# Second attention: the value products of a key tile in two halves by queries, one half in each step, and the output copies one step later

## The chip, the cores and the metric

The kernel runs on one core of a Trainium2 chip. The metric is the device time of one launch in microseconds. TensorE is called PE (its weight loads PEld), VectorE DVE, ScalarE ACT, GpSimd POOL, and SyncE SP; SP and ACT also issue DMAs.

## The reference

Two layers over x of 4 x 512 tokens with 256 features, in fp32. Each layer is x + attention(xn) + ffn(xn), with xn the layer-normalised x. Layer 0 has single-head attention and a mixture of 16 experts (4 per token) with a shared one; layer 1 has the grouped attention below and a mixture of 7 experts (3 per token) with a shared one. The change is in the second attention alone:

```
fused = x @ w_qkv.T + b_qkv            # q: 32 heads of 8; k, v: 8 groups of 8, 4 heads to a group
sim   = einsum('bgrsd,bgtd->bgrst', q, k) / sqrt(8)
attn  = softmax(sim, axis=-1)          # 512 queries x 512 keys, for 4 x 8 groups of 4 heads
out   = einsum('bgrst,bgtd->bgrsd', attn, v)
out   = out.reshape(B, S, 256) @ w_out.T + b_out
```

## The kernel before, in words

Every engine has its own hand-written program; semaphores order them. A unit u is one batch and one group of four heads (4 x 8 = 32 units, NG = 8 units to a batch). The work on a unit is spread over three stages, so that in stage u PE computes the scores of unit u (for their maxima), the transposed scores of unit u-1 (and the last three of u-2), and value products of units u-2 and u-1. A stage has eight steps i, one for each pair of heads in a tile of 128 queries or keys (QT = 4 tiles, 2 pairs).

In each step, in this order on PE:

- `scores_t` (L846): two 32-row products of 512 columns into two PSUM banks, keys by queries, with the maxima folded into the queries (`qm`). ACT's `exponentials` (L1200) turns the two banks into half a tile of `pt`. It runs LAG = 3 steps behind, so steps 0 to 2 still do unit u-2.
- `scores` (L834): two 32-row products of 512 columns into two banks, queries by keys; DVE's `reduce_max` (L1691) takes the maxima out.
- in step 1 `maxima_t` (L873): four 128 x 128 transposes of the negated maxima; DVE then adds them to the queries of the next unit (L1694, gives b_qm). scores_t of unit u-1 begins in step 3 and waits for that.
- in steps 0, 2 and 4 `values` (L858) of the key tiles 1, 2, 3 of unit u-2, and in step 6 of tile 0 of unit u-1: four products of all 128 keys by 512 queries, one for each head, side by side in column groups of 32, accumulated in PSUM bank 7. `va` holds the values with a column of ones, so a row of sums comes out as well.
- in step 3 a projection of the next batch in the stages u % 8 = 5, 6, 7 of all batches but the last (`project`, L563 to L565, six products of 512 columns); ACT (L1179 to L1184) and DVE (L1653, L1656) `compact` it, ACT in its step 4, DVE in step 5.
- in step 4 of stages 9, 17 and 25 `values_by_key` (L823), four transposes, which DVE copies to `va` (L1660).
- in step 6 `outputs_t` (L866): four transposes of `ot`, from which DVE normalises the result (L1668, L1670).

ACT's `outputs` (line 1191, recorded at the helper's line L1000) copies bank 7 to `ot` in ACT's step 4, when the value products of unit u-2 are complete. outputs_t waits for it (b_ot), and so do the first value products of the next unit, which overwrite bank 7.

The banks of both kinds of scores come from a ring of three slots of two banks: `next_slot` lets the n-th use wait for the reader of the use three before. So scores(i) waits for the exponential of scores_t(i-1), and scores_t(i) for the reduction of scores(i-2). PSUM bank 6 (SMALL) is shared by maxima_t, project, values_by_key and outputs_t: `small_bank` lets each wait for the reader of the one before. `pt` is a ring of three key tiles: `exponentials` waits on b_pv until the products of the tile three before are complete.

SP's `stack_keys` and `stack_queries` (L392, L407) bring keys and queries of later units into place by DMA, waiting on b_st and b_qm; POOL scatters tokens to the experts (L482), three scatters for each maxima_t in stages 13 to 28. In stages 3 to 7, 9 and 10 DVE also does the routing of layer 1.

Of the kernel before, what the change touches and what calls it, by code (L numbers as in the profile page):

```python
# [8 lines left out]
B, S, H = 4, 512, 256  # L9
# [3 lines left out]
QT = S // P  # L13
# [16 lines left out]
NG, R, HD = 8, 4, 8  # L30
# [11 lines left out]
def program(nc, x_in, aw0_in, aw1_in, ws0_in, moe0_in, moe1_in, pad_in, const_in, bias_in, out):  # L42
# [3 lines left out]
    with ctx:  # L46
        i32, u32 = mybir.dt.int32, mybir.dt.uint32

        def place(name, col, shape, dt=f32):
            return nc.alloc_sbuf_tensor_at(name, shape, dt, offset=SBUF0 + 4 * col)  # L50

        def sem(name):
            return ctx.enter_context(nc.semaphore(name))
# [76 lines left out]
        psum = ctx.enter_context(nc.psum_tensor("psum", [P, 8, 512], f32))  # L130
# [64 lines left out]
        va = tf(QT, NG, 32)  # L195
        pt = [tf(R, S), tf(R, S), place("pt2", M + 32848, [P, R, S])]
# [60 lines left out]
        b_pv, b_ot, b_ox, b_rc, b_on, b_nt = (sem(n) for n in ("b_pv", "b_ot", "b_ox", "b_rc", "b_on", "b_nt"))  # L257
# [34 lines left out]
        UNITS, PAIRS, LAG = B * NG, 2 * QT, 3  # L292
# [3 lines left out]
        def projects(u):  # L296

            return NEXT.get(u % NG) if u < UNITS - NG else None

        def new_values(u):  # L300

            return u % NG == 1 and NG < u < UNITS
# [258 lines left out]
        def _(pe):  # L561
# [276 lines left out]
            def scores_t(u, i):  # L838

                t, h = i // 2, i % 2  # L840
                if i == 0:
                    pe.wait_ge(b_qm, u + 1)
                bank = next_slot(pe, ("scores_t", u, i), b_ex, u * PAIRS + i + 1)
                for r in range(2):
                    rows = slice(32 * (2 * h + r), 32 * (2 * h + r) + 32)
                    ins = nc.tensor.matmul(psum[:, bank + r, :], km[u % 4][rows, t * P:(t + 1) * P],  # L846
                                           qm[u % 2][rows, :], start=True, stop=True, tile_position=(32 * (2 * h + r), 0))
                ins.then_inc(b_st, 1)

            def values(u, t):  # L850

                pe.wait_ge(b_ex, u * PAIRS + 2 * t + 2)
                if t == 0 and u >= 1:
                    pe.wait_ge(b_ot, u)
                if t == 0 and u % NG == 0:
                    pe.wait_ge(b_va, u // NG + 1)
                for r in range(R):
                    ins = nc.tensor.matmul(psum[32 * r:32 * r + 32, 7, :], va[:, t, u % NG, :], pt[(u * QT + t) % 3][:, r, :],  # L858
                                           start=(t == 0), stop=(t == QT - 1), tile_position=(0, 32 * r))
                ins.then_inc(b_pv, 1)  # L860

            def outputs_t(u):
# [15 lines left out]
            def stage(u, early={}):  # L878

                front = u < UNITS  # L880
                if front:
                    pe.wait_ge(b_kd, (u + 1) * R * 16)
                    pe.wait_ge(b_qd, (u + 1) * R * 16)
                for i in range(PAIRS):
                    if i < LAG and u >= 2:
                        scores_t(u - 2, PAIRS - LAG + i)
                    if i >= LAG and 1 <= u <= UNITS:
                        scores_t(u - 1, i - LAG)
                    if front:
                        scores(u, i)  # L890
                    if i == 1 and 1 <= u <= UNITS:
                        maxima_t(u - 1)
                    if i % 2 == 0 and i < 6 and u >= 2:
                        values(u - 2, 1 + i // 2)
                    if i == 3 and projects(u) is not None:
                        project(projects(u), u // NG + 1, small_bank(pe, b_lo, u // NG * 3 + u % NG - (NG - 3) + 4))
                    if i == 4 and new_values(u):
                        values_by_key(small_bank(pe, b_va, u // NG + 1))
                    if i == 5 and u == NG:
                        prefix(1, small_bank(pe, m_tot, layers(1, 1)))  # L900
                    if i == 6 and 2 <= u <= UNITS:
                        outputs_t(u - 2)
                    if i == 6 and 1 <= u <= UNITS:
                        values(u - 1, 0)
                    if i in early:
                        early[i]()

# [60 lines left out]
            for t in range(QT):  # L968
                ins = nc.tensor.transpose(psum[:, 7, t * P:(t + 1) * P], ot[:, t * P:(t + 1) * P], ident)
            ins.then_inc(b_ox, 1)  # L970
            attention_t(2)
            for b in range(B):
# [5 lines left out]
                for i in range(KH):  # L978
                    ins = to_tokens(2 * b, on_hi[:, i, tok], on_lo[:, i, tok], w1_hi[1][:, i, :], w1_lo[1][:, i, :],
                                    i == 0, i == KH - 1)  # L980
# [17 lines left out]
        def _(act):  # L998
# [161 lines left out]
            for b in range(B):  # L1160
                for k in (2, 3):
                    r = k * T + b * S
# [22 lines left out]
                    ins.then_inc(b_hi, 1)  # L1185

            def outputs(u):
                act.wait_ge(b_pv, (u + 1) * QT)
                if u >= 1:
                    act.wait_ge(b_ox, u)  # L1190
                copy(ot[:], psum[:, 7, :]).then_inc(b_ot, 1)

            def exponentials(u, i):

                t, h = i // 2, i % 2
                act.wait_ge(b_st, u * PAIRS + i + 1)
                if u * QT + t >= 3:
                    act.wait_ge(b_pv, u * QT + t - 2)
                bank = slots["scores_t", u, i]
                nc.scalar.activation(pt[(u * QT + t) % 3][:, 2 * h:2 * h + 2, :], psum[:, bank:bank + 2, :],  # L1200
                                     ACT.Exp, scale=float(HD) ** -0.5).then_inc(b_ex, 1)

            def stage(u):
                for i in range(PAIRS):
                    if u == 2 and i == 2:
                        gating_exp(E1, 2, TT)
                    if i < LAG and u >= 2:
                        exponentials(u - 2, PAIRS - LAG + i)
                    if i >= LAG and 1 <= u <= UNITS:
                        exponentials(u - 1, i - LAG)  # L1210
                    if i == 4 and projects(u) is not None:
                        compact(projects(u), u // NG + 1, psum[:, SMALL, :], u % NG - (NG - 3))
                    if i == 4 and u >= 2:
                        outputs(u - 2)


# [43 lines left out]
        def _(dve):  # L1260
# [414 lines left out]
            def stage(u, early={}):  # L1675
                front = u < UNITS
                for i in range(PAIRS):
                    if 3 <= u < NG:
                        next(to_mask1, None)
                        next(to_mask1, None)  # L1680
                    if u == NG and i == 6:
                        place_totals(1, psum[:, SMALL, :])
                    if u == NG + 1:
                        next(to_slots1, None)
                        next(to_slots1, None)
                    if i == 5 and projects(u) is not None:
                        compact(projects(u), u // NG + 1, psum[:, SMALL, :], u % NG - (NG - 3))
                    if front:
                        bank = slots["scores", u, i]
                        dve.wait_ge(b_sn, u * PAIRS + i + 1)  # L1690
                        v.reduce_max(mx[:, u % 2, 2 * i:2 * i + 2], psum[:, bank:bank + 2, :], AX.X).then_inc(b_mx, 1)  # L1691
                    if i == 1 and 1 <= u <= UNITS:
                        dve.wait_ge(b_mt, u)
                        v.tensor_tensor(qm[(u - 1) % 2], psum[:, SMALL, :], qs[(u - 1) % 4].bitcast(f32),  # L1694
                                        ALU.add).then_inc(b_qm, 1)
                    if i == 4 and new_values(u):
                        values_by_key(u // NG, psum[:, SMALL, :])
                    if i == 6 and 2 <= u <= UNITS:
                        normalise(u - 2, psum[:, SMALL, :])
                    if i in early:  # L1700
                        early[i]()
                if front:

                    dve.wait_ge(b_mx, (u + 1) * PAIRS)
                    if u >= 1:
                        dve.wait_ge(b_mt, u)
                    m = mx[:, u % 2, :].rearrange("p (t r) -> p t r", r=R)
                    z = mz[:].rearrange("p t (r c) -> p t r c", c=32)[:, :, :, 24:26]
                    v.tensor_scalar(z[:, :, :, 0], m, -1.0, None, ALU.mult).then_inc(b_m1, 1)
                    dve.wait_ge(b_m1, u + 1)  # L1710
                    v.scalar_tensor_tensor(out=z[:, :, :, 1], in0=m, scalar=-1.0, in1=z[:, :, :, 0].bitcast(f32),
                                           op0=ALU.mult, op1=ALU.subtract).then_inc(b_m2, 1)
# [159 lines left out]
```

## Time and profile before

| | before |
|---|---|
| median of 3 runs | 1146.82 us (1143.93 to 1152.62) |
| the profiled execution's own time | 1146.65 us |
| its span (first to last instruction) | 1144.9 us |
| mean granted TensorE clock | 0.931 |
| PE busy | 945.5 us (83%) |
| DVE busy | 744.4 us (65%) |
| ACT busy | 595.3 us (52%) |
| POOL busy | 317.6 us (28%) |

The busy times are sums over the whole span, over parts with different limits. The second attention's stages begin at 442.71 us (first scores) and end with the last normalisation at about 930 us. A stage is told here by the time from its first L834 to that of the next stage.

### The profile page before, as it was taken

To read this page: it belongs to the slowest core of one execution; us is meant where nothing else is said; L and a number is where in the kernel's file an instruction comes from. 1 tells how busy PE (TensorE), PEld (TensorE's weight loads), DVE (VectorE), ACT (ScalarE), POOL (GpSimd) and SP (SyncE) were. 2 spreads that over 40 slices of the span, in tenths; PEclk is the share of its full clock that TensorE was granted. 3 is DMA by queue.
4 is the path that set the end of the run, shared out by engine and by line. 5 is a ranking of instruction groups with operands and counts; after the bars stand their busy time and mean duration, and the time that the engine had idled before them with its cause. 6 is when DMAs were issued, how large, how long until landed. Compare 5 with 4: busy or idle time off the path is not lost.

```text
span 1144.9 us, 17381 instructions
## 1 busy us (share of the span) xinstructions
PE 945.5 (83%) x5780; PEld 637.5 (56%) x5780; DVE 744.4 (65%) x1335; ACT 595.3 (52%) x913; POOL 317.6 (28%) x331
## 2 busy tenths in 40 slices
PE   4999994769999845788877888888888887999996
PEld 3877873659999723423322333233222265888885
DVE  6577553556655346589688877887788846434437
ACT  6325553355565523366565656665566665444431
POOL 2005777066655500000000111221221000455441
PEclk9999998889999967689799979998899998999998
DMA  6862333364444273011111212332232125333253
GB/s 228 315 273 111 121 112 117 104 201 146 133 127 134 93 298 52 3 27 30 21 32 23 48 37 53 66 68 45 49 66 59 51 65 160 108 107 99 92 200 132
DMA packets 49651, 120.48 MB, mean 105 GB/s; under 512 B 8264, under 2 KB 25416, under 8 KB 49032
## 3 DMA queue, kind: packets, MB, share of 16 engines
q1 hardware_dynamic: 36608, 82.80, 25.2%
q0 software_dynamic: 11808, 32.37, 7.5%
q10 hardware_dynamic: 1152, 4.19, 0.9%
q8 instruction: 52, 0.85, 0.3%
q14 instruction: 31, 0.25, 0.1%
HBM read 72.30 MB, written 52.42 MB: 109 GB/s over the span
## 4 chain that ended last, share of the span: by engine, by line
PE 59%; ACT 12%; DVE 11%; POOL 7%; issue 6%; DMA 4%; SPq 0%; ACTq 0%; DVEq 0%; POOLq 0%
PE psum L858 11%; ACT work_f L1200 6%; POOL xg L482 5%; PE psum L846 5%; PE psum L834 5%; PE psum L649 5%; PE psum L650 4%; PE psum L651 4%; PE psum L563 3%; PE psum L565 3%; PE psum L564 3%; ACT pt L1200 3%; DVE work_f L1691 3%; PE psum L635 3%; PE psum L660 2%
## 5 line engine op out<-in xcount | busy, mean ns | idle before, releaser
L1691 DVE TENSOR_REDUCE work_f<-psum 128x2 f32<-128x1024 f32 x256 | 312.2, 1221 | 67.3 <-PE psum L834 63.9
L1200 ACT ACTIVATE work_f<-psum 128x1024 f32<-128x1024 f32 x172 | 170.2, 1026 | 103.4 <-PE psum L846 103.2
L489 POOL DMA_INDIRECT yk<-yb,dest x134 | 130.8, 976 | 236.1 <-ACT yb L1060 212.6
L482 POOL DMA_INDIRECT xg<-xn,slot x112 | 108.2, 966 | 183.6 <-PE psum L873 145.0
L846 PE MATMUL psum<-work_r 32*128 32x512 f32 x512 | 122.3, 508 | 10.3 <-DVE work_f L1691 7.5
L846 PEld LDWEIGHTS psum<-work_r 32*128 32x128 f32 x512 | 47.7, 195 | 148.0 <-DVE work_f L1691 60.2
L1200 ACT ACTIVATE pt<-psum 128x1024 f32<-128x1024 f32 x84 | 83.3, 1027 | 52.5 <-PE psum L846 52.5
L649 PE MATMUL psum<-wexp,xbh 128*128 x268 | 102.5, 382 | 7.4 <-issue 6.3
L858 PE MATMUL psum<-work_f 128*32 128x512 f32 x688 | 100.2, 657 | 1.2 <-ACT work_f L1200 1.2
L834 PE MATMUL psum<-work_r,qs_more 32*128 32x512 f32 x256 | 68.6, 532 | 38.5 <-ACT work_f L1200 25.0
L834 PE MATMUL psum<-work_r 32*128 32x512 f32 x256 | 67.4, 538 | 37.9 <-ACT work_f L1200 20.7
L650 PE MATMUL psum<-wexp,xbh 128*128 x268 | 96.4, 360 | 0.0
L651 PE MATMUL psum<-wexp,xbl 128*128 x268 | 96.1, 358 | 0.0
L1045 ACT ACTIVATE sgb<-psum 128x352 f32<-128x352 f32 (+1 forms) x67 | 34.8, 519 | 98.6 <-PE psum L651 98.6
L1479 DVE TENSOR_TENSOR xbl<-psum,xbh 128x512 fp32r<-128x512 f32 x67 | 46.3, 690 | 57.1 <-ACT xbh L1000 56.8
L1060 ACT ACTIVATE yb<-psum,share 128x256 f32<-128x256 f32 x134 | 56.3, 471 | 47.6 <-PE psum L677 24.0
L478 POOL TENSOR_TENSOR xn<-const 128x16 f32<-128x16 f32 x7 | 1.5, 218 | 270.4 <-PE psum L873 194.0
L1489 DVE TENSOR_TENSOR hb<-sgb,psum 128x352 f32<-128x352 f32 (+1 forms) x67 | 39.1, 584 | 51.4 <-ACT sgb L1045 51.3
L649 PEld LDWEIGHTS psum<-wexp,xbh 128*128 128x128 f32 x268 | 52.0, 194 | 13.8 <-issue 10.1
L834 PEld LDWEIGHTS psum<-work_r 32*128 32x128 f32 x256 | 24.8, 196 | 60.1 <-ACT work_f L1200 34.6
L834 PEld LDWEIGHTS psum<-work_r,qs_more 32*128 32x128 f32 x256 | 25.2, 194 | 58.1 <-ACT work_f L1200 39.4
L635 PE MATMUL psum<-const,xb 128*128 128x128 f32 x268 | 42.2, 282 | 15.9 <-DVE xbl L1479 10.2
(222 smaller groups left out, 2178.2 us busy)
## 6 DMA issues: line engine op xcount, KB each, us to landing
xb<-xg SPq DMA_DIRECT2D x67, 258.0 KB
xg<-in_pad SPq DMA_DIRECT2D x1, 10320.0 KB
yg<-yk SPq DMA_DIRECT2D x20, 512.0 KB, 9.1
stage<-in_moe SPq DMA_DIRECT2D x16, 608.0 KB, 4.3
work_r<-work_r SPq DMA_DIRECT2D x192, 48.0 KB
xg<-in_pad SPq DMA_DIRECT2D x1, 7224.0 KB
stage<-in_moe SPq DMA_DIRECT2D x16, 384.0 KB, 3.8
yg<-yk ACTq DMA_DIRECT2D x8, 512.0 KB, 12.6
```

The lines of the kernel that those rows point to most:

```text
L482: nc.gpsimd.indirect_dma_start(xg[l], bass.IndirectOffsetOnAxis(ap=slot[l][:, at:at + 1], axis=0), xn[l][:, t, :], None).then_inc(m_scat, 16)
L489: nc.gpsimd.indirect_dma_start(yk[l], bass.IndirectOffsetOnAxis(ap=dest[:, j % 8, i:i + 1], axis=0), yb[l][:, j % 2, i, :], None).then_inc ...
L635: ins = nc.tensor.transpose(psum[:, 4, (i * KH + c) * P:(i * KH + c + 1) * P], xb[l][:, j % 2, i, c * P:(c + 1) * P], ident)
L649: nc.tensor.matmul(o, xbh[l][:, j % 2, i * KH + c, :], hi, start=c == 0, stop=False)
L650: nc.tensor.matmul(o, xbh[l][:, j % 2, i * KH + c, :], lo, start=False, stop=False)
L651: ins = nc.tensor.matmul(o, xbl[l][:, j % 2, i * KH + c, :], hi, start=False, stop=c == KH - 1)
L834: ins = nc.tensor.matmul(psum[:, bank + r, :], qs[u % 4][rows, t * P:(t + 1) * P], km[u % 4][rows, :], start=True, stop=True, tile_positio ...
L846: ins = nc.tensor.matmul(psum[:, bank + r, :], km[u % 4][rows, t * P:(t + 1) * P], qm[u % 2][rows, :], start=True, stop=True, tile_positio ...
L858: ins = nc.tensor.matmul(psum[32 * r:32 * r + 32, 7, :], va[:, t, u % NG, :], pt[(u * QT + t) % 3][:, r, :], start=(t == 0), stop=(t == QT ...
L1060: ins = nc.scalar.activation(yb[l][:, j % 2, i, :], psum[:, 6, i * H:(i + 1) * H], ACT.Identity, scale=share[:, j % 8, i:i + 1])
L1200: nc.scalar.activation(pt[(u * QT + t) % 3][:, 2 * h:2 * h + 2, :], psum[:, bank:bank + 2, :], ACT.Exp, scale=float(HD) ** -0.5).then_inc( ...
L1691: v.reduce_max(mx[:, u % 2, 2 * i:2 * i + 2], psum[:, bank:bank + 2, :], AX.X).then_inc(b_mx, 1)
```

## The change

A key tile's value products are made in two halves by queries. The four products of 512 queries become four of queries 0 to 255 in one step and four of queries 256 to 511 in the next, so that each of the eight steps has one half: steps 0 to 5 for the key tiles 1 to 3 of unit u-2, steps 6 and 7 for tile 0 of unit u-1. b_pv counts halves, and the waits on it are doubled to match. ACT's copy of the outputs moves from its step 4 to step 5, and so does values_by_key, on PE and on DVE. The order within a step stays: scores_t, scores, maxima_t, values, project, values_by_key, outputs_t, values of the next unit. Nothing changes for SP and POOL.

```diff
-            def values(u, t):
+            def values(u, n):
+                t, half = n // 2, slice(n % 2 * (S // 2), (n % 2 + 1) * (S // 2))
                 pe.wait_ge(b_ex, u * PAIRS + 2 * t + 2)
-                if t == 0 and u >= 1:
+                if n == 0 and u >= 1:
                     pe.wait_ge(b_ot, u)
...
                 for r in range(R):
-                    ins = nc.tensor.matmul(psum[32 * r:32 * r + 32, 7, :], va[:, t, u % NG, :], pt[(u * QT + t) % 3][:, r, :],
-                                           start=(t == 0), stop=(t == QT - 1), tile_position=(0, 32 * r))
+                    ins = nc.tensor.matmul(psum[32 * r:32 * r + 32, 7, half], va[:, t, u % NG, :],
+                                           pt[(u * QT + t) % 3][:, r, half],
+                                           start=(n == 0), stop=(n == 2 * QT - 1), tile_position=(0, 32 * r))
                 ins.then_inc(b_pv, 1)
...
-                    if i % 2 == 0 and i < 6 and u >= 2:
-                        values(u - 2, 1 + i // 2)
+                    if i < 6 and u >= 2:
+                        values(u - 2, 2 + i)
...
-                    if i == 4 and new_values(u):
+                    if i == 5 and new_values(u):
                         values_by_key(small_bank(pe, b_va, u // NG + 1))
...
-                    if i == 6 and 1 <= u <= UNITS:
-                        values(u - 1, 0)
+                    if i >= 6 and 1 <= u <= UNITS:
+                        values(u - 1, i - 6)
...
             def outputs(u):
-                act.wait_ge(b_pv, (u + 1) * QT)
+                act.wait_ge(b_pv, (u + 1) * 2 * QT)
...
                 if u * QT + t >= 3:
-                    act.wait_ge(b_pv, u * QT + t - 2)
+                    act.wait_ge(b_pv, 2 * (u * QT + t - 2))
...
-                    if i == 4 and u >= 2:
+                    if i == 5 and u >= 2:
                         outputs(u - 2)
...
-                    if i == 4 and new_values(u):
+                    if i == 5 and new_values(u):
                         values_by_key(u // NG, psum[:, SMALL, :])
```

## Rows read from the trace of the kernel before

**Rows 1.** The page: busy tenths, granted clock, in 40 slices of 28.6 us.

```profile
PE   4999994769999845788877888888888887999996
...
PEclk9999998889999967689799979998899998999998
```

**Rows 2.** Stretches: us, busy PE, PEld, DVE, ACT, POOL (count); clock, DMA, GB/s.

```profile
505.27:518.12 12.85, 10.36 (x73) 3.64 (x74) 12.64 (x35) 8.46 (x10) 0.00 (x0) 1.00 0.21 32
622.46:635.29 12.83, 10.45 (x73) 3.63 (x73) 11.04 (x14) 8.35 (x10) 0.00 (x0) 1.00 0.20 33
...
680.00:698.21 18.21, 15.53 (x78) 5.83 (x78) 11.87 (x15) 9.49 (x12) 2.88 (x3) 0.73 0.25 54
...
711.05:724.38 13.33, 10.87 (x78) 3.98 (x78) 11.46 (x15) 8.45 (x10) 2.88 (x3) 1.00 0.27 59
...
750.08:762.92 12.84, 10.45 (x72) 3.63 (x72) 11.04 (x14) 8.35 (x10) 2.88 (x3) 1.00 0.28 63
...
914.20:930.50 16.30, 14.08 (x110) 6.07 (x109) 3.02 (x7) 14.32 (x18) 0.00 (x0) 1.00 0.00 1
```

**Rows 3.** The chain that ended last, in stage 20: start us, us, what.

```profile
752.04 1.03 ACT work_f L1200
753.08 0.04 issue
```

**Rows 4.** Timeline of stage 20: start us, us, engine, line, shapes, count, idle before.

```profile
753.12 0.50 PE L834 MATMUL psum<-work_r 32*128 32x512 f32 x2
753.23 0.68 DVE L1694 TENSOR_TENSOR work_r<-psum,qs_more 128x512 fp32r<-128x512 f32 x1
753.55 0.16 PEld L858 LDWEIGHTS psum<-pt,work_f 128*32 128x32 f32 x8 [0.25 <-issue]
753.55 1.06 PE L858 MATMUL psum<-pt,work_f 128*32 128x512 f32 x8
...
754.55 0.50 PE L846 MATMUL psum<-work_r 32*128 32x512 f32 x2
...
755.09 1.94 ACT L1200 ACTIVATE work_f<-psum 128x1024 f32<-128x1024 f32 x2 [1.00 <-PE psum L846]
...
757.73 0.59 ACT L1000 COPY work_f<-psum 128x512 f32<-128x512 f32 x1 [0.70 <-PE psum L858]
...
758.22 1.95 ACT L1200 ACTIVATE pt<-psum 128x1024 f32<-128x1024 f32 x2
...
759.72 0.66 PE L866 MATMUL psum<-const,work_f 128*128 128x128 f32 x4
...
760.31 1.07 PE L858 MATMUL psum<-work_f 128*32 128x512 f32 x8
```

**Rows 5.** Timeline of PE: products of 512 and of 256 columns back to back.

```profile
768.40 0.40 PE L565 MATMUL psum<-xt_hi,aw 128*128 128x512 f32 x1
768.63 0.39 PE L563 MATMUL psum<-xt_hi,aw 128*128 128x512 f32 x1
...
936.36 0.28 PE L563 MATMUL psum<-aw,on_hi 128*128 128x256 f32 x1
936.48 0.29 PE L564 MATMUL psum<-aw,on_hi 128*128 128x256 f32 x1
```

**Rows 6.** Timeline of PE in stage 21, a projection stage.

```profile
767.83 0.50 PE L563 MATMUL psum<-xt_hi,aw 128*128 128x512 f32 x1
...
769.41 0.50 PE L846 MATMUL psum<-work_r 32*128 32x512 f32 x2
...
773.59 0.50 PE L834 MATMUL psum<-work_r 32*128 32x512 f32 x2 [1.81 <-ACT work_f L1200]
```

**Rows 7.** Timeline of PE in stage 6, steps 0 to 2.

```profile
546.61 1.94 PE L858 MATMUL psum<-pt,work_f 128*32 128x512 f32 x8
548.48 0.79 PE L846 MATMUL psum<-work_r 32*128 32x512 f32 x2
...
550.82 1.07 PE L858 MATMUL psum<-work_f 128*32 128x512 f32 x8
```

More of the change, by code:

```diff
@@ L848, in scores_t @@
                 ins.then_inc(b_st, 1)
-            def values(u, t):
+            def values(u, n):
+                t, half = n // 2, slice(n % 2 * (S // 2), (n % 2 + 1) * (S // 2))
                 pe.wait_ge(b_ex, u * PAIRS + 2 * t + 2)
-                if t == 0 and u >= 1:
+                if n == 0 and u >= 1:
                     pe.wait_ge(b_ot, u)
-                if t == 0 and u % NG == 0:
+                if n == 0 and u % NG == 0:
                     pe.wait_ge(b_va, u // NG + 1)
                 for r in range(R):
-                    ins = nc.tensor.matmul(psum[32 * r:32 * r + 32, 7, :], va[:, t, u % NG, :], pt[(u * QT + t) % 3][:, r, :],
-                                           start=(t == 0), stop=(t == QT - 1), tile_position=(0, 32 * r))
+                    ins = nc.tensor.matmul(psum[32 * r:32 * r + 32, 7, half], va[:, t, u % NG, :],
+                                           pt[(u * QT + t) % 3][:, r, half],
+                                           start=(n == 0), stop=(n == 2 * QT - 1), tile_position=(0, 32 * r))
                 ins.then_inc(b_pv, 1)
```

## The prediction

> **What bounds the kernel now.** I read the page's slices first: from 443 to 930 us the kernel is in the second attention, PE stands at 7 to 8 tenths, and the granted clock falls below full in several slices [rows 1]. No engine is full, so the stage is held by a chain of waits. The stretches show how it repeats: one stage (eight steps, eight pairs of heads' scores) follows another, and a plain stage takes 12.84 us with DVE busy 11.04, PE 10.45 and ACT 8.35 [rows 2]. Eleven stages are like that (11, 12, 16, 18 to 20, 26 to 30; two of them are shown).
>
> The chain of waits inside stage 20 names what holds it [rows 3]. Call s(i) the scores of step i, st(i) its transposed scores, v the value products of a key tile. The chain goes: exponential 1.03, hand-off 0.05, s 0.43 until the next instruction starts (753.12 to 753.55 [rows 4]), v 1.00 (753.55 to 754.55), st 0.54 until ACT can start (754.55 to 755.09). The sum is 3.05 us for two steps, which is the distance of two such pieces (750.08, where the stage begins, to 753.12). Every second step holds the whole v, and the next st, on whose exponential everything waits, is queued behind it on PE. The step between has no v: there, maxima_t (four transposes, 0.59 by those of outputs_t) lies hidden, since s(2) waits for ACT anyway until 753.12. A plain stage is 4 x 3.05 + 0.59 for outputs_t, which does lie on the chain (759.72 to 760.31), + about 0.05 = 12.84.
>
> **The change part by part.** *The half product.* It removes no work: 4 products of 512 queries become 2 x 4 of 256. I need h, the time from the start of a half to the next instruction. No half is in the trace, so I bound it. Lower end: half of 1.00, 0.50. Upper end: no shrinking at all, 1.00. Nearest rows: three-product groups with 512 columns start every 0.23 us, with 256 columns every 0.12 [rows 5]; streaming halves with the width, with about 0.01 left over. The whole v is two passes: s, one pass of 512 columns, takes 0.43, so 2 x 0.43 = 0.86 of the 1.00 streams and 0.14 is fixed. That gives h = 0.43 + 0.14 = 0.57, so each tile costs PE 0.14 more than before. PE pays this in every step, but the chain then holds 0.57 where it held 1.00.
>
> The fixed 0.14 is seen at the exit: v to st takes 1.00, two passes of 0.43 and a remainder, while s to v shows nothing beyond 0.43. The Trainium skill (TensorEngine Tiling, "Key Properties") says that changing the tiling mode, not only the tile, drains TensorE; the change doubles the crossings between 32x128 and 128x32 tiles. If no such cost came twice, h would be 0.50 and the stage 0.3 us shorter still.
>
> *The new pair of steps.* Every step is now s, half v, st. From one s to the one two steps later: 0.43 + 0.57 + 0.54 + 1.03 + 0.05 = 2.62 instead of 3.05. Two such chains run side by side (even and odd steps), for 4 x 2.62 = 10.48 a stage each. maxima_t loses its cover, since its step now holds a half too: chain one is 10.48 + 0.59 = 11.07. outputs_t is on chain two: 10.48 + 0.59 = 11.07, plus the copy, below.
>
> *outputs(u-2) a step later.* The last half is in step 5, so the copy, 0.59 long and releasing ACT after 0.48 (757.73 to 758.22), comes behind exp(5). Queued behind it on ACT is the exponential of step 6, and outputs_t on PE waits for the copy. The half of step 5 ends about when exp(5) does, so the copy starts 0.1 to 0.2 late and ends just after PE has finished s(6): outputs_t waits 0.1 to 0.2, and the half of step 6 and st(7) behind it. Chain two becomes 11.2 to 11.3. The chains are not independent (ACT and PE run in order): following st, s and exp step by step with these durations, and the 0.68 of the query update between reductions, gives 11.35 to 11.45.
>
> *DVE.* It is busy 11.04 of a stage whatever PE does, and has some eight hand-offs; 0.4 of idleness is the least I expect, so DVE alone says 11.4. st(3) waits for the query update: reduce(1) starts 0.54 after s(1), takes 1.22, the update 0.68 (they overlap by 0.08), so st(3) can go 2.4 us after s(1); PE comes to it at 1.00 + 0.59 + 1.00 = 2.6. That wait stays covered by 0.2 us, unless DVE is late. With three limits at 11.1 to 11.45 I take 11.6 for the plain stage: a gain of 1.25.
>
> *values_by_key a step later* and the waits of `exponentials` on b_pv: the product of the tile three earlier is now complete two steps before it is needed, not three, and lies ahead of that step's st on PE; nothing. values_by_key adds 0.5 to its three stages as before (13.33 against 12.84, stage 17 [rows 2]). Nothing is issued by SP or POOL in the moved steps; SP's stacking waits for scores, POOL for maxima_t, both of them earlier.
>
> *Projection stages* (nine: 5 to 7, 13 to 15, 21 to 23). Six products take 1.58 us (767.83 to 769.41 [rows 6]) in step 3. Before they filled a step without v and cost the chain 0.4; now they follow a half and cost it about 1.3. In return the compact on ACT (1.14 until the next can start) no longer has outputs queued directly between it and exp(5), and s(6) comes 0.5 sooner. Stage 21 would be 14.3 at full clock now; I get 13.7 to 14.1 and take a gain of 0.5.
>
> *Stages where DVE is full.* Stage 3 has DVE busy 12.64 of 12.85 [rows 2] and stage 4 is alike: 0.6 together. Stages 9 and 10 are busy with the routing as well: 0.5 together.
>
> *The clock.* Some 65 us of this part run at a granted 0.5, that is 1.2 of 2.4 GHz: slices with 6 to 8 [rows 1], stage 15 at 0.73 and 18.21 us [rows 2]. There v takes 1.87 (546.61 to 548.48), and from one v to the next two steps later it is 4.21 (546.61 to 550.82) [rows 7] in place of 3.05. A half at that clock is 1.07 (the same 0.57 of the whole), so a pair gains 0.8 instead of 0.43: for 65 / 4.2 = 15 pairs 5 us more. The falls follow the long stands of PE in projection stages: 1.81 us before 773.59 [rows 6], with the fall at 775. That stand shrinks to about 0.6, so one or two falls fewer, 2 us more.
>
> **The sum.** 11 plain stages x 1.25 = 13.8; stages 3, 4: 0.6; stages 8, 17, 25: 3.0; 9 and 10: 0.5; nine projection stages x 0.5 = 4.5; stages 1, 2, 24, 31: 4.0; the clock: 7; the two stages without scores at the end (from 914.20, ACT busy 14.32 of 16.30 [rows 2]): 0.5. Together 33.9. The profiled execution took 1146.65 us (span 1144.9), within 0.2 of the median 1146.82: 1146.65 - 33.9 = 1112.8, say **1113**.
>
> **The rivals.**
> 1. *DVE becomes the bound and its lateness comes back through the query update.* For it: 11.04 of 12.84 busy, and the cover at st(3) is 0.2. Against: reductions have three slots to lag in. If st(3) waits 0.5 us in each stage and the chain does not make it up, a plain stage gives 0.6 and a projection stage 0: about 16 us gain, 1130.
> 2. *Twice as many small instructions.* A plain stage now issues 72 products and as many weight loads [rows 2], 11 instructions to a microsecond; it would issue 104 of each, 18 to a microsecond. Today the eight weight loads of v take 0.16 us together, beside their products [rows 4]. If in a half so short they came out from beside them, h grows by 0.16: pairs of 2.78, a plain stage near 12.3, 32 stages x 0.64 = 20 us less gain, 1133. The Trainium skill (TensorEngine Tiling, "Instruction Overhead") gives about 60 cycles of overhead for each matmul; the trace of v doesn't show that as a serial cost, with eight in 1.00 us of which 0.86 streams.
> 3. *The half does not shrink (slower).* If a 256-column pass in 128x32 tiles costs what the 512 one does, h = 1.00: pairs stay at 3.05, maxima_t is uncovered (0.6) and the copy wait stays (0.2): 13.7 a plain stage, +0.85 x 30 = 25 us, 1172. It decides against the change from about h = 0.88, where four pairs take back the 1.25. Against it: 0.23 to 0.12 [rows 5].
> 4. *The clock takes it back.* The stands of PE in projection stages grow instead, with 1.3 us of products moved out of cover, and the low clock holds whole stages: 20 us of gain plainly, and 20 us of lows more: 1147.
> 5. *The lows vanish* as PE becomes denser (10.5 of 12.84 busy now, about 10.9 of 11.6 after): what the lows cost now, some 20 us in all, comes back instead of 7: 1100.
>
> **How the numbers follow.** Forecast (1105 to 1121) 0.52; DVE 0.16; small instructions 0.06; half not shrinking 0.07; clock 0.07; lows vanish 0.12. Faster by over 1% (under 1135, about what a measurement of this kernel can tell from no change): 0.52 + 0.12 + most of 0.22 = 0.82; slower by over 1% 0.07, rounded to 0.08; within 0.10. The range takes in the fast case with h = 0.50 and reaches past the two slower gains: 1096 to 1140; what is left out is half not shrinking, the clock case and tails.
>
> **What would show it.** Plain stages at 11.4 to 11.8 with all eight s evenly spaced near 1.3 us, in place of 1.43 and 1.61; half v to st at 0.57; DVE idle under 0.6 a stage; outputs_t a short wait for the copy (ACT L1000); st(3) starting right behind the half. Wrong if h is above 0.8, if L846 waits for L1694 in most stages, if projection stages get longer, or if the slices from 491 to 900 us show more low clock than now.

## The result and the profile after

The changed kernel takes 1134.77 us (median of 6 runs, 1132.1 to 1138.73), the kernel before 1150.73 in its own six (1143.93 to 1156.29): a ratio of 0.988, 95% interval 0.9847 to 0.9914. That is faster by 1.2%, where 2.9% was forecast; 1134.77 lies inside the forecast range of 1096 to 1140, and the gain is under half of the 34 us. The profiled execution took 1137.07 us with a span of 1135.3. The two profiled executions (1146.65 and 1137.07) lie 9.6 us apart, not the 16 us of the medians; the rows below compare these two.

The page of the changed kernel has PE denser, and the clock of the same slices no better than in [rows 1]:

```profile
PE   4998898769999926689998989999999996999996
...
PEclk9999999889999968678988987997889998999999
```

Its stretches, one stage each (12, 15, 18, 20, 26, 27) and then stages 11 to 30 together, with the columns of [rows 2]:

```profile
633.37:644.75 11.38, 10.84 (x104) 4.22 (x104) 10.76 (x14) 8.66 (x10) 0.00 (x0) 1.00 0.23 36
674.08:693.63 19.55, 18.86 (x112) 7.60 (x113) 11.78 (x15) 9.61 (x11) 2.88 (x3) 0.59 0.30 55
720.25:731.63 11.38, 10.79 (x104) 4.19 (x104) 10.63 (x14) 8.65 (x10) 3.29 (x5) 1.00 0.33 71
743.98:756.36 12.38, 11.13 (x104) 4.35 (x105) 10.84 (x14) 8.55 (x10) 2.87 (x3) 1.00 0.26 66
830.80:844.43 13.63, 12.76 (x104) 4.92 (x105) 10.93 (x14) 8.60 (x9) 2.87 (x3) 0.82 0.31 59
844.43:858.23 13.80, 12.99 (x106) 4.84 (x107) 11.13 (x14) 8.60 (x10) 2.88 (x3) 0.81 0.29 59
621.86:894.48 272.62, 254.96 (x2126) 101.05 (x2124) 222.76 (x269) 179.67 (x195) 47.35 (x54) 0.89 0.26 58
```

Stages of one kind no longer agree. Stage 12 and 18 take 11.38 us, better than the 11.6 forecast for a plain stage; stage 20 takes 12.38 at the same full clock; 26 and 27 take 13.6 and 13.8 at 0.82 and 0.81, and stage 15 19.55 at 0.59, against 18.21 at 0.73 in [rows 2]. Before the change every plain stage took 12.84. In the kernel before stages 11 to 30 took 279.92 us at a mean clock of 0.94; now they take 272.62 at 0.89. At a mean of 0.89, 2 x 0.11 of the stretch, about 60 us, is at the half clock, against about 34 before.

The timeline of stage 20 of the changed kernel shows the extra microsecond (L846 are the transposed scores, L834 the scores, L859 the half products, L1202 the exponentials, L1693 the reductions):

```profile
747.02 0.64 PE L859 MATMUL psum<-pt,work_f 128*32 128x256 f32 x8
...
747.59 0.50 PE L846 MATMUL psum<-work_r 32*128 32x512 f32 x2
747.62 0.96 POOL L482 DMA_INDIRECT xg<-xn,slot  x1 [0.30 <-issue]
...
748.47 1.02 ACT L1202 ACTIVATE work_f<-psum 128x1024 f32<-128x1024 f32 x1 [0.33 <-PE psum L846]
...
748.88 0.96 POOL L482 DMA_INDIRECT xg<-xn,slot  x1 [0.30 <-issue]
...
749.20 0.50 PE L846 MATMUL psum<-work_r 32*128 32x512 f32 x2
...
750.73 1.02 ACT L1202 ACTIVATE work_f<-psum 128x1024 f32<-128x1024 f32 x1 [1.24 <-PE psum L846]
750.77 1.22 DVE L1693 TENSOR_REDUCE work_f<-psum 128x2 f32<-128x1024 f32 x1 [0.81 <-PE psum L834]
```

The half is what was forecast: 747.02 to 747.59, 0.57. But the transposed scores that begin at 749.20 release ACT only at 750.73, 1.53 us later instead of the 0.54 of [rows 4]; those of 747.59 release it after 0.88. ACT and DVE, which wait for different products, both start at 750.7: PE's results come late, while PE's own records go on at their normal distances. It happens beside POOL's scatters (L482), which follow each other every 1.26 us from step 1 on. Stages 12, 29 and 30 have no scatters, and stage 18 has one early and two 7.0 us behind its start; all four take 11.4.

### The profile page after: what moved, and what is told of

Read it like the earlier page. It is cut to its first block, busy times and chain, and to the rows that moved or that the text cites. A ratio compares the mean times of both kernels' runs of the same rounds, so it can differ in the third digit from the quotient of the medians.

```text
span 1135.3 us, 19429 instructions
## 1 busy us (share of the span) xinstructions
PE 988.1 (87%) x6804; PEld 667.7 (59%) x6804; DVE 740.7 (65%) x1335; ACT 603.3 (53%) x913; POOL 317.2 (28%) x331
## 4 chain that ended last, share of the span: by engine, by line
PE 59%; DVE 15%; ACT 8%; POOL 7%; issue 6%; DMA 4%; SPq 0%; ACTq 0%; DVEq 0%; POOLq 0%
PE psum L859 9%; PE psum L846 7%; DVE work_f L1693 5%; POOL xg L482 5%; PE psum L649 5%; PE psum L650 4%; PE psum L651 4%; PE psum L563 3%; ACT work_f L1202 3%; PE psum L834 3%; PE psum L564 3%; PE psum L565 3%; PE psum L635 3%; PE psum L660 2%; PE psum L868 2%
## 5 line engine op out<-in xcount | busy, mean ns | idle before, releaser
L1693 DVE TENSOR_REDUCE work_f<-psum 128x2 f32<-128x1024 f32 x256 | 307.6, 1219 | 59.9 <-PE psum L834 55.8
L1202 ACT ACTIVATE work_f<-psum 128x1024 f32<-128x1024 f32 x172 | 175.9, 1026 | 99.3 <-PE psum L846 98.4
L482 POOL DMA_INDIRECT xg<-xn,slot x112 | 108.1, 965 | 181.9 <-PE psum L875 145.1
L846 PE MATMUL psum<-work_r 32*128 32x512 f32 x512 | 141.0, 547 | 9.4 <-DVE work_f L1693 4.5
L846 PEld LDWEIGHTS psum<-work_r 32*128 32x128 f32 x512 | 51.8, 199 | 131.7 <-issue 75.9
L859 PE MATMUL psum<-work_f 128*32 128x256 f32 x1376 | 122.5, 432 | 0.1
L1202 ACT ACTIVATE pt<-psum 128x1024 f32<-128x1024 f32 x84 | 86.1, 1026 | 48.8 <-PE psum L846 48.6
L834 PE MATMUL psum<-work_r 32*128 32x512 f32 x256 | 69.7, 556 | 14.4 <-ACT work_f L1202 5.3
L834 PE MATMUL psum<-work_r,qs_more 32*128 32x512 f32 x256 | 72.2, 560 | 10.3 <-ACT work_f L1202 5.0
L859 PE MATMUL psum<-pt,work_f 128*32 128x256 f32 x672 | 60.3, 434 | 0.0
L651 PEld LDWEIGHTS psum<-wexp,xbl 128*128 128x128 f32 x268 | 52.4, 195 | 5.0
```

The lines of the kernel that those rows point to most:

```text
L482: nc.gpsimd.indirect_dma_start(xg[l], bass.IndirectOffsetOnAxis(ap=slot[l][:, at:at + 1], axis=0), xn[l][:, t, :], None).then_inc(m_scat, 16)
L651: ins = nc.tensor.matmul(o, xbl[l][:, j % 2, i * KH + c, :], hi, start=False, stop=c == KH - 1)
L834: ins = nc.tensor.matmul(psum[:, bank + r, :], qs[u % 4][rows, t * P:(t + 1) * P], km[u % 4][rows, :], start=True, stop=True, tile_positio ...
L859: ins = nc.tensor.matmul(psum[32 * r:32 * r + 32, 7, half], va[:, t, u % NG, :], pt[(u * QT + t) % 3][:, r, half], start=(n == 0), stop=(n ...
```

## The experiments

**1. The scatters after the last stage.** What separates the good stages from the bad ones was moved away, in the changed kernel and in the one before.

```diff
-                    if 0 <= u < TT:
-                        for i in range(TOP1):
-                            dispatch(1, u * TOP1 + i)
+            for n in range(TT * TOP1):
+                dispatch(1, n)
```

> The changed kernel with POOL's 48 scatters of layer 1 after the last maxima_t instead of three a stage in stages 13 to 28 (the end grows by some 60 us). Theory A (POOL's scatters delay the completion of PE's products, which costs a stage 1.0 us and makes the clock fall): all plain stages from 11 to 30 take 11.4 us, no product of stages 13 to 30 completes more than 0.2 us late, and the low clock of 620 to 900 us falls from some 60 us to 30 or less. Theory B (the late completions come from PE's own denser stream of instructions): stages 19, 20, 26, 28 stay at 12.3 and more and the lows stay.

> The kernel before with the same move of the scatters. Both theories: plain stages stay at 12.84 us, since none of its products completed late. Against the changed kernel with the same move, theory A expects the stretch of stages 11 to 30 to be shorter by 25 us or more; theory B by about the 12 us it is now.

The changed kernel so altered (1163.62 us with the longer end), its stages 15, 20, 26 and then 11 to 30:

```profile
673.29:687.04 13.75, 12.89 (x111) 5.41 (x111) 11.28 (x15) 9.60 (x12) 0.00 (x0) 1.00 0.32 49
733.04:744.43 11.39, 10.83 (x105) 4.21 (x106) 10.76 (x14) 8.66 (x10) 0.00 (x0) 1.00 0.22 37
809.46:820.85 11.39, 10.81 (x105) 4.20 (x106) 10.76 (x14) 8.65 (x10) 0.00 (x0) 1.00 0.23 36
620.64:866.34 245.70, 232.21 (x2126) 93.53 (x2127) 219.88 (x269) 180.16 (x195) 0.00 (x0) 0.99 0.22 38
```

The kernel before so altered (1203.97 us), stages 20 and 11 to 30:

```profile
755.63:768.48 12.85, 10.44 (x74) 3.64 (x74) 11.05 (x14) 8.36 (x10) 0.00 (x0) 1.00 0.20 33
626.60:903.82 277.22, 226.35 (x1485) 82.20 (x1486) 225.71 (x269) 175.35 (x195) 0.00 (x0) 0.96 0.20 34
```

Theory A holds. Without scatters every plain stage from 12 on takes 11.4, the clock of the stretch is 0.99, and the change is worth 277.22 - 245.70 = 31.5 us in these twenty stages instead of 279.92 - 272.62 = 7.3 (not the 12 that the expectation gave). Part of the 31.5 is clock (0.99 beside 0.96), and each kernel was run once. Theory B, PE's denser stream alone, falls: the stream is the same here. The two kernels differ by 40 us (1163.62 and 1203.97): 6 us more lie before stage 11 and 3 behind stage 30.

**2. The scatters four steps later, and both halves in one step.** The first moves what is suspected; the second splits a tile without interleaving it.

```diff
+                        pool.wait_ge(b_st, (u + 12) * PAIRS + 3)
                         for i in range(TOP1):
                             dispatch(1, u * TOP1 + i)
```

> The changed kernel with the three scatters of a stage waiting for the transposed scores of step 5 instead of maxima_t of step 1. Theory A: the late products move with them, from steps 2 to 4 to steps 5 to 7 of stages 13 to 28; the time changes little either way (within 4 us of the changed kernel, 1135). Theory B: late products stay in steps 2 to 4.

It measured 1130.83 us (1123.38 to 1147.94 in ten runs), ratio 0.9874 (0.9835 to 0.9913). The late results moved: in stage 19 of this kernel (L1203 are the exponentials, L847 the transposed scores) it is step 7 that ends late.

```profile
731.72 0.96 POOL L482 DMA_INDIRECT xg<-xn,slot  x1 [0.30 <-issue]
...
732.99 0.96 POOL L482 DMA_INDIRECT xg<-xn,slot  x1 [0.30 <-issue]
...
733.71 0.50 PE L847 MATMUL psum<-work_r 32*128 32x512 f32 x2
734.77 1.94 ACT L1203 ACTIVATE pt<-psum 128x1024 f32<-128x1024 f32 x2 [2.35 <-PE psum L847]
```

From 733.71 to 734.77 it is 1.06 instead of 0.54, and the next scores wait for ACT until 735.85.

```diff
-                    if i < 6 and u >= 2:
-                        values(u - 2, 2 + i)
+                    if i % 2 == 0 and i < 6 and u >= 2:
+                        values(u - 2, 2 + i)
+                        values(u - 2, 3 + i)
...
-                    if i >= 6 and 1 <= u <= UNITS:
-                        values(u - 1, i - 6)
+                    if i == 6 and 1 <= u <= UNITS:
+                        values(u - 1, 0)
+                        values(u - 1, 1)
```

(outputs and values_by_key back in step 4.)

> The split alone: both halves of a tile in the even step, outputs and values_by_key in step 4 as in the kernel before. Theory of the forecast (a half costs 0.57, two 1.14, the chain holds both): plain stages 12.84 + 4 x 0.14 = 13.4 us, the kernel some 16 us over before. If the two halves run without the second entry (0.50 each): 12.9. Theory A says few or no late products, if it takes the denser interleaving to meet them; theory B says late products here too, since there are as many instructions.

Its stage 20, PE and the stretch:

```profile
759.40 1.07 PE L859 MATMUL psum<-work_f 128*32 128x256 f32 x16
760.40 0.50 PE L846 MATMUL psum<-work_r 32*128 32x512 f32 x2
```

```profile
758.97:771.84 12.87, 10.52 (x104) 4.67 (x105) 10.94 (x14) 8.35 (x10) 2.88 (x3) 1.00 0.28 63
```

13.4 was expected and 12.87 measured (the kernel 1153.21 in one run, beside a median of 1147.37). Two halves in a row take 1.00 together, as the whole tile did: the split costs nothing, and the 0.14 is paid only where PE leaves the 128x32 products for another kind. (In a projection stage the next products are 128x128, and a half takes 0.57 up to them too: 750.74 to 751.31 in the kernel of experiment 3.) The Trainium skill (TensorEngine Tiling (Array Packing), "Key Properties") says that changing the tiling mode drains TensorE; these rows agree at that exit. This kernel has as many PE instructions as the changed one, 208 in 12.87 us or 16 to a microsecond, and its results are late too. Here are the scores of step 3 in stage 20 and the reduction that waits for them (L1695):

```profile
763.46 0.50 PE L834 MATMUL psum<-work_r 32*128 32x512 f32 x2
...
764.54 2.36 DVE L1695 TENSOR_REDUCE work_f<-psum 128x2 f32<-128x1024 f32 x2 [0.60 <-PE psum L834]
```

From 763.46 to 764.54 it is 1.08 us; in the kernel before, and in this kernel's stages without scatters, it is 0.58. Stage 20 and twelve others of the sixteen with scatters show this. The chain doesn't wait for these scores, so the plain stages were not lengthened, except 18 (15.03 us) and 24 (13.79). So theory B had this part right. The late results need the scatters, but they come with the split itself, which doubles the instructions of the value products, and not only with the interleaving. Whether a stage pays for them depends on what its chain waits for.

**3. The scatters apart.**

```diff
                         for i in range(TOP1):
+                            pool.wait_ge(b_st, (u + 12) * PAIRS + 2 * i + 1)
                             dispatch(1, u * TOP1 + i)
```

> The changed kernel with a stage's three scatters set apart: they wait for the transposed scores of steps 3, 5 and 7 instead of following each other from step 1 on. If it is the closeness of the scatters that delays products, the single ones delay little and stages 16 to 28 come near 11.4 us, the kernel at 1118 to 1125. If each scatter delays by itself, products are late by 0.7 us or more three times a stage and the time stays at 1130 to 1137.

It measured 1110.77 us (1110.21 to 1121.69) against 1146.96: ratio 0.9715, interval 0.9659 to 0.977. That is under the 1118 to 1125 expected. Its stages 15, 20, 27 and 11 to 30:

```profile
674.93:688.68 13.75, 12.89 (x110) 5.41 (x110) 11.29 (x15) 9.60 (x12) 2.88 (x4) 1.00 0.41 79
...
734.71:746.10 11.39, 10.82 (x104) 4.21 (x105) 10.86 (x14) 8.66 (x10) 2.88 (x4) 1.00 0.29 72
...
822.51:833.90 11.39, 10.83 (x106) 4.22 (x106) 10.86 (x14) 8.68 (x10) 2.87 (x4) 1.00 0.32 73
622.28:868.03 245.75, 232.50 (x2127) 93.92 (x2127) 220.43 (x269) 180.16 (x195) 47.28 (x54) 0.99 0.29 64
```

All 48 scatters are in that stretch (POOL 47.28 busy), and it takes what it took without them. So it is not scatters beside PE, but scatters close behind each other.

The control is the same pacing in the kernel before, where tiles are whole:

> The control: the kernel before, whole tiles, with a stage's scatters set apart (steps 3, 5, 7) as in the fast version. If close scatters only hurt the denser kernel, its ratio to the kernel before is 1.00 within 0.01 and plain stages stay at 12.84. If pacing is a gain of its own, it gives some of the 1.6 points between the changed kernel (0.988) and the paced one (0.9715) here too.

1147.93 us against 1147.27, ratio 1.0013 (0.9979 to 1.0047): pacing alone is worth nothing.

**4. How close is close.** In the changed kernel, two scatters from step 3 on, one in step 7 (`(1, 1, 5)[i]` in place of `2 * i + 1`).

> The changed kernel with two scatters from step 3 on, one behind the other, and the third in step 7. If a scatter right behind another one is what delays PE, the second still gives one late group in a stage and plain stages of 11.4 to 12; if it takes three in a row, stages of 11.4. In the changed kernel the delays ended near the end of the second and 0.8 after that of the third.

1118.69 us in one run. Stages 20, 27 and 11 to 30:

```profile
732.72:744.23 11.51, 11.22 (x104) 4.38 (x104) 10.48 (x14) 8.54 (x10) 2.87 (x4) 1.00 0.30 71
818.59:830.09 11.50, 11.24 (x104) 4.40 (x104) 10.49 (x14) 8.54 (x10) 2.87 (x4) 1.00 0.33 69
621.25:875.87 254.62, 242.45 (x2128) 97.75 (x2126) 220.41 (x269) 179.20 (x195) 47.35 (x54) 0.95 0.28 62
```

A plain stage loses 0.12 us to a pair, and 1.0 to three in a row; of the stages with values_by_key, 17 took 12.39 and 25 took 12.76, against 11.84 for 25 in the paced kernel. So a second scatter can be enough, and a third makes it much larger. Where the pair falls counts as well. In stage 24 of the kernel of experiment 3 two scatters also follow each other at once:

```profile
794.92 0.96 POOL L482 DMA_INDIRECT xg<-xn,slot  x1 [6.37 <-PE psum L847]
796.18 0.96 POOL L482 DMA_INDIRECT xg<-xn,slot  x1 [0.30 <-issue]
```

They begin 7.0 us into the stage, and it took 11.38, as stage 18 of the changed kernel did. Nor is the whole difference to the kernel of experiment 3, 254.62 against 245.75, the pairs: 8.4 us of it are in stages 22 to 24, which hold 24 us at half clock.

**5. What of a scatter does it.** The scatters last again, and in their place three plain DMAs of POOL a stage, or three additions of POOL; both are extra work whose results nothing reads.

```diff
+                            nc.gpsimd.dma_start(trial[...], xn[1][:, u, 0:H]).then_inc(m_trial, 16)
```

> The changed kernel with the scatters last, and in their place in stages 13 to 28 three plain DMAs each, issued by POOL, of a tile of 128 tokens x 256 columns from the same xn to a scratch tensor in HBM. If the data traffic of a POOL queue or its reading of xn delays PE, products are late here as well and plain stages take 12.3. If it takes the scatter's own work (an index for each row, descriptors made at run time), plain stages take 11.4.

```diff
+                            nc.gpsimd.tensor_tensor(trial[:, n % 2, :], xn[1][:, u, 0:H], xn[1][:, u, 0:H], ALU.add).then_inc(m_trial, 1)
```

> The changed kernel with the scatters last, and in their place in stages 13 to 28 three additions of 128 x 256 on POOL each, on data of the same xn. If POOL's use of SBUF or of its port is what delays PE, late products and stages of 12 us and more; if it is DMA, plain stages at 11.4 us.

Stage 20 took 11.39 and 11.38 us. The kernel with additions, stages 15, 20, 27 and 11 to 30:

```profile
673.43:693.00 19.57, 18.88 (x112) 7.61 (x112) 11.78 (x15) 9.62 (x11) 1.75 (x3) 0.59 0.22 35
741.21:752.59 11.38, 10.80 (x104) 4.18 (x104) 10.76 (x14) 8.66 (x10) 1.76 (x3) 1.00 0.22 37
821.36:832.75 11.39, 10.84 (x106) 4.22 (x106) 10.77 (x14) 8.67 (x10) 1.76 (x3) 1.00 0.23 36
620.41:878.27 257.86, 244.81 (x2126) 97.77 (x2126) 221.57 (x269) 180.14 (x195) 28.08 (x48) 0.93 0.21 36
```

Neither these additions nor plain DMAs of nearly the same size make PE late, so it is most likely something of the indirect DMA itself. It is not shown to the end: three additions take POOL 1.76 us and three plain DMAs 1.61, one right behind the other, where three scatters take 2.88 and stretch over 3.5 us, so they stand beside fewer of PE's products. These two kernels show a second thing: without a single late result, stage 15 takes 19.57 at a clock of 0.59, and the stretch 257.86 where it took 245.70. The clock can fall around projection stages in one of these kernels and not in another with the same work there; here that is worth 12 us.

**6. The copy of the outputs left in step 4** (scatters last).

```diff
-                    if i == 5 and u >= 2:
+                    if i == 4 and u >= 2:
                         outputs(u - 2)
```

> The changed kernel with the scatters last, and ACT's copy of the outputs left in its step 4, where it waits for the half of PE's step 5 and holds up the exponential of step 5. The copy's move is needed if plain stages grow by 0.5 us or more over the 11.38 with the copy in step 5 (exp(5) then starts after the half of step 5, some 0.7 later, and s(6) with it). Rival: no difference, since outputs_t gets its copy earlier: 11.4.

```profile
879.44 0.50 PE L833 MATMUL psum<-work_r,qs_more 32*128 32x512 f32 x2
...
880.45 0.50 PE L845 MATMUL psum<-work_r 32*128 32x512 f32 x2
880.58 0.59 ACT L1001 COPY work_f<-psum 128x512 f32<-128x512 f32 x1 [1.19 <-PE psum L858]
881.06 1.95 ACT L1201 ACTIVATE pt<-psum 128x1024 f32<-128x1024 f32 x2
882.15 0.50 PE L833 MATMUL psum<-work_r,qs_more 32*128 32x512 f32 x2 [1.21 <-ACT pt L1201]
```

ACT stands 1.19 us in front of the copy while the exponential of step 5 could run, and the scores of step 6 come 2.71 us after those of step 5 (879.44 to 882.15) instead of 1.0. Every stage has such a stand of PE, stages 11 to 30 take 306.9 us at a mean clock of 0.81, and the kernel 1250.61. The move of the copy, forecast as a cost of 0.1 to 0.2, is a condition of the change.

## Why the prediction was wrong

*What held.* The reading of the chain was right, and so was h: 0.57. The undisturbed plain stage takes 11.38 where 11.35 to 11.45 was worked out (11.6 was taken, for caution). Undisturbed projection stages take 13.75, inside 13.7 to 14.1, and 14.3 in the middle one of each three. The eight scores are not evenly spaced: they come 1.0 to 1.9 us apart, and only the pair of steps is as forecast (2.62). st(3) starts right behind the half, so rival 1 didn't come. outputs_t waits 0.3 for the copy (740.44 + 0.43 to 741.21) instead of 0.1 to 0.2. With the scatters apart the whole sum comes out: 36 us between the medians (1146.96 - 1110.77) against 34. That this fits so well is partly luck. A plain stage gains 1.46 and not 1.25, the half clock in stages 11 to 30 falls from 34 us to 4, and stages 4 and 9, at half clock in part, lose 1.3 and 1.9 us where a gain was taken.

*The step that failed* is the sentence "Nothing is issued by SP or POOL in the moved steps", taken to mean that they cost nothing. POOL's scatters stayed where they were, beside steps that now have a half each. In stage 20 of the kernel before:

```profile
752.88 0.96 POOL L482 DMA_INDIRECT xg<-xn,slot  x1 [9.35 <-PE psum L873]
754.14 0.96 POOL L482 DMA_INDIRECT xg<-xn,slot  x1 [0.30 <-issue]
755.40 0.96 POOL L482 DMA_INDIRECT xg<-xn,slot  x1 [0.30 <-issue]
```

PE beside them became denser, from 11 to 18 instructions to a microsecond, and three scatters in a row then make PE's results late by 0.3 and 1.0 us in one stage. The trace of before had the same scatters beside whole tiles without a late result, so it gave no row for this. The rival on small instructions had the right suspect, their number, but looked at the weight loads: h stayed at 0.57.

*The clock* was the second wrong term, a gain of 7 forecast. The prediction's own sign came: between 491 and 900 us the half clock went from 56 us to 96. A late microsecond is a stand of PE. In stage 26 the late results come at step 4, and ACT starts 1.0 us late; from 839.5 us on the products run at half clock:

```profile
836.01 0.50 PE L846 MATMUL psum<-work_r 32*128 32x512 f32 x2
...
837.55 1.02 ACT L1202 ACTIVATE work_f<-psum 128x1024 f32<-128x1024 f32 x1 [1.23 <-PE psum L846]
...
839.70 0.79 PE L846 MATMUL psum<-work_r 32*128 32x512 f32 x2
```

Stages 24 and 28 have the same, and 25 and 27 begin in what is left of it. Stages 11 to 30 had about 60 us of half clock, the paced kernel (experiment 3) about 5. Of the 26.9 us between the two in these stages, the late microseconds themselves are some 8, by estimate (stages 13, 17, 19, 20, 26, 28 and parts of others); the rest is clock. Not all of that rest can be put down to the scatters. Some 24 us of the half clock are in stages 24 to 28, where each fall stands behind a late result. Another 24 are in stages 14 to 16, and the kernels of experiment 5 have the same 24 there with no late result at all; they took 12 us more than the undisturbed kernel. The stages before 11, which have no scatters, vary in the same way: stage 4 took 14.15 us in the changed kernel with its clock fallen, and 12.21 at full clock in the kernel with additions, with the same waits of PE for DVE. In the kernel before it took 12.84, and stages 3 and 4 were to gain 0.6 together.

*The rivals.* Number 4 named the clock as what takes the gain back, and its direction was right, but by longer stands in projection stages; undisturbed those are shorter. Number 3 didn't come. Number 5, the lows vanish, didn't come in the changed kernel, but nearly did in stages 11 to 30 of the paced one (34 us of half clock before, 4 there).

*Open.* What in an indirect DMA delays PE's results, and whether it is the making of descriptors or its packets; and what the records of PE mean, whose starts stay on time while the results are late. That kernels with halves are hit and kernels with whole tiles are not is shown (experiments 2, 3 and its control); why is not. Nor does any run show whether the recording itself takes part. The trace of the changed kernel lacks 10 of the 256 rises of the semaphore behind the scores, all beside scatters; with the scatters last it lacks none, and in the kernel before none.

## What to carry to other kernels

Splitting a long product so that each step of a software pipeline holds an equal share shortens the chain that waits behind it, and the split itself is free where the halves stay in one tiling mode. When an engine gets denser, look at every other engine's work beside it again, also at what the change doesn't touch: here the gain of 36 us was there, and some 19 of it (ratios 0.988 and 0.9715) hung on setting three indirect DMAs apart, which was worth nothing before. Stages of one kind that no longer agree in their time are the place to look, sorted by what else runs in each.

## What was not expected of the hardware

Three indirect DMAs of POOL 1.26 us apart made results of a PE with 16 to 18 instructions to a microsecond late by 0.3 to 1.0 us, and not those of one with 11. Two cost a stage 0.12 (up to 0.9 beside values_by_key) when they began 4.9 us into it and nothing at 7.0 us; single ones, plain DMAs and additions of POOL cost nothing. Two back-to-back halves of 256 columns in 128x32 tiles took 1.00 us, as one of 512 did. A stand of PE of about one microsecond in a stage was followed by a fall of the granted clock in some stages (26, 28) and not in others (19, 20).
